# Two attention layers on one core: projections issued in halves over separate slots, the second transposes one slot after the norm, the router three slots earlier

## The reference, cut to what matters

```python
x = x + tanh(g_xattn[0]) * attention0(layernorm(x), ctx, mask)   # q from x, k and v from ctx
x = x + tanh(g_ffn[0])   * quantised_ffn(layernorm(x))           # fake-quantised, 768 wide
x = x + tanh(g_xattn[1]) * attention1(layernorm(x), ctx)
x = x + tanh(g_ffn[1])   * top1_moe(layernorm(x))                # 32 experts, 160 rows each
```

## Time and profile before

| | us |
|---|---|
| median of 3 executions | 1279.54 (1276.82 to 1281.15) |
| the profiled execution: its time | 1276.96 |
| its span, first to last instruction | 1275.7 |
| PE busy | 1202.8 (94% of the span) |
| DVE busy | 893.2 (70%) |
| ACT busy | 709.5 (56%) |
| POOL busy | 480.2 (38%) |

### The profile page before, as it was taken

The page is one execution under the profiler, slowest core; times in us unless marked ns, Lnnn a source line. Parts: engine busy times, 40 slices in busy tenths (PEclk is TensorE's granted clock), DMA queues, the critical chain, the costliest instruction groups (busy, mean ns, idle before and its releaser), DMA issues.

```text
span 1275.7 us, 25161 instructions
## 1 busy us (share of the span) xinstructions
PE 1202.8 (94%) x9252; PEld 861.7 (68%) x9252; DVE 893.2 (70%) x2680; ACT 709.5 (56%) x1197; POOL 480.2 (38%) x677
## 2 busy tenths in 40 slices
PE   7799999999999989999999998999999999989998
PEld 6567677767777664444448875777677677668987
DVE  4677777876787646589999955777877868652333
ACT  2355555555655538889984425666566666632221
POOL 5434434443443100057100434444544643323555
PEclk9899999999999989999999999999999999999999
DMA  7523334333432032000003654446456342148973
GB/s 187 136 61 111 96 93 117 89 101 99 125 92 68 11 108 76 1 1 2 1 1 116 173 149 121 128 114 183 126 163 150 106 132 83 52 147 253 306 193 36
DMA packets 121941, 137.22 MB, mean 108 GB/s; under 512 B 12881, under 2 KB 116427, under 8 KB 121797
## 3 DMA queue, kind: packets, MB, share of 16 engines
q1 hardware_dynamic: 111888, 125.98, 33.4%
q0 software_dynamic: 7296, 8.15, 3.5%
q10 hardware_dynamic: 2634, 1.49, 0.5%
HBM read 58.42 MB, written 27.36 MB: 67 GB/s over the span
## 4 chain that ended last, share of the span: by engine, by line
PE 56%; DVE 6%; issue 3%; ACT 2%; POOL 1%; DMA 1%; ACTq 0%; SPq 0%; POOLq 0%; DVEq 0%
PE PS L670 14%; PE PS L729 6%; PE PS L471 5%; PE PS L411 5%; PE PS L684 4%; PE PS L430 4%; PE PS L454 4%; PE PS L503 2%; PE PS L738 2%; PE PS L529 2%; PE PS L418 2%; DVE NM L1133 1%; PE PS L547 1%; ACT P L853 1%; PE PS L512 1%
## 5 line engine op out<-in xcount | busy, mean ns | idle before, releaser
L853 ACT ACTIVATE P<-PS 128x512 f32<-128x512 f32 x512 | 302.5, 602 | 162.5 <-PE PS L457 88.4
L1130 DVE CUSTOM_DVE_ANT_0 MX<-PS,NQ 128x256 bf16<-128x256 f32 x512 | 192.4, 418 | 72.1 <-PE PS L430 72.0
L454 PE MATMUL PS<-QS,KS 99*128 99x256 bf16 x1024 | 226.1, 274 | 8.1 <-ACT P L853 7.1
L1133 DVE TENSOR_REDUCE NM<-PS 128x2 f32<-128x512 f32 x256 | 173.6, 686 | 71.0 <-PE PS L430 69.4
L430 PE MATMUL PS<-KS,QS 96*128 96x256 bf16 x1024 | 196.4, 274 | 23.2 <-DVE NM L1130 14.7
L430 PEld LDWEIGHTS PS<-KS,QS 96*128 96x128 bf16 x1024 | 86.6, 97 | 89.0 <-DVE NM L1130 26.9
L471 PE MATMUL PS<-P,V 128*32 128x256 f32 x2048 | 138.4, 388 | 1.5 <-ACT P L853 1.5
L454 PEld LDWEIGHTS PS<-QS,KS 99*128 99x128 bf16 x1024 | 95.9, 99 | 50.7 <-ACT P L853 20.9
L457 PE MATMUL PS<-NK,identb 128*128 128x256 bf16 x512 | 128.0, 275 | 0.0
L670 PE MATMUL PS<-XNT,wup 128*128 128x512 f16 x576 | 124.9, 379 | 0.0
L670 PEld LDWEIGHTS PS<-XNT,wup 128*128 128x128 f16 x576 | 56.1, 98 | 67.4
(11 more groups left out here) (240 smaller groups left out, 2479.5 us busy)
## 6 DMA issues: line engine op xcount, KB each, us to landing
KS<-PP SPq DMA_DIRECT2D x192, 128.0 KB, 3.0
QS<-PP SPq DMA_DIRECT2D x192, 128.0 KB, 2.5
WH<-in_wex SPq DMA_DIRECT2D x16, 768.0 KB, 8.3
WG<-in_wex SPq DMA_DIRECT2D x10, 768.0 KB, 5.4
bufd<-bias_row SPq DMA_DIRECT2D x5, 1032.0 KB, 11.8
XB<-in_x SPq DMA_DIRECT2D x16, 256.0 KB, 3.1
CT<-in_ctxT SPq DMA_DIRECT2D x16, 256.0 KB, 3.1
x1d<-XB SPq DMA_DIRECT2D x16, 256.0 KB, 2.1
```

What stands on the lines that cost most here:

```text
L454: ins = tensor.matmul(o, t.KS[b % 3][0:99, h, 128 * kt:128 * kt + 128], t.QS[b % 3][0:99, h, :], start=True, stop=(L == 1))
L853: scalar.activation(t.P[h % 8][:, :, :], PS[:, h % 2, :].rearrange("p (k n) -> p k n", k=2), ACT.Exp).then_inc(s_ex, 1)
L1130: ins = vector.tensor_tensor_reduce(t.MX[:, 2 * (h % 2) + qt, :], PS[:, bk, 256 * qt:256 * qt + 256], t.NQ[b % 4][:, qt, :], -1.0, 1.0e30, ...
L1133: ins = vector.tensor_reduce(nm[:, :, h], PS[:, bk, :].rearrange("p (t n) -> p t n", t=2), X, ALU.max, negate=True)
```

## The change: what it does

For all sequences but the first two of a layer:

| job | slot before | slot after |
|---|---|---|
| keys | 0 | half in 0, half in 2 |
| rows | 1 | 3 |
| queries | 3 | half in 7, half in 8 |
| values | 13 | half in 12, half in 14 |
| DVE rounding of keys, queries | 2, 5 | 4, 10 |
| SP copies of the keys' parts | 2, 3 | 4, 5 |
| SP copies of the queries' parts | 4, 6 | 10, 11 |

For all sequences:

| job | slot before | slot after |
|---|---|---|
| out | 10 | half in 10, half in 11 |
| residual, statistics, moments | 10, 11, 12 | 11, 12, 13 |
| power on POOL | 12 | 13 |
| the two norm instructions | 13 and 14 | both in 14 |
| second transposes | 4 of the next but one `s` | 15 of the next `s` |
| router | 7 | 4 |
| heads | 5 and 6 | both in 6 (DVE: 6 and 7) |

Between its two halves a job keeps its bank, and the jobs between go to the other one. The preparation of the FFN's weights moves from slots 0, 3, 5 (of each 8) to 3, 4, 7. Before the experts, `pe_warm_mixed` becomes 30 of the plain unread matmuls. No arithmetic changes. The diff, cut to its core:

```diff
+def keys_at(b):
+    return (0, 0) if b < 2 else (0, 2)
+def rows_at(L, b):
+    return 3 if b >= 2 else 0 if rows_first(L, b) else 1
+def queries_at(b):
+    return (3, 3) if b < 2 else (7, 8)
+def values_at(b):
+    return (13, 13) if b < 2 else (12, 14)
+def mids_at(L, b):
+    return (4, 10) if b >= 2 else (2, 8 if (L, b) == (0, 1) else 5)
+def stacks_at(L, b):
+    return ((4, 5), (10, 11)) if b >= 2 else ((2, 3), (4, mids_at(L, b)[1] + 1))
...
-        def odd_bank(job, emptier, value):
+        def odd_bank(job, emptier, value, half=None):
+            if half == 1:
+                half_done.remove(home[job])
+                return home[job]
             turn[0] ^= 1
+            if 6 + turn[0] in half_done:
+                turn[0] ^= 1
             bk = 6 + turn[0]
+            if half == 0:
+                half_done.add(bk)
             if emptied[bk] is not None:
                 pe.wait_ge(*emptied[bk])
...
-                if k in (5, 6):
-                    pe_heads(L, s - 1, k - 5)
+                if k == 6:
+                    pe_heads(L, s - 1, 0)
+                    pe_heads(L, s - 1, 1)
...
-                    pe_out(L, s - 1)
+                    pe_out(L, s - 1, 0)
+                if k == 11:
+                    pe_out(L, s - 1, 1)
+                if k == 15:
+                    if s == NB:
+                        pe_warm(5, 14)
+                    pe_xm(L, s - 1)
             if 0 <= s - 2 < NB:
-                if k == 4:
-                    if s - 2 == NB - 1:
-                        pe_warm(5, 14)
-                    pe_xm(L, s - 2)
-                if L == 1 and k == 7:
+                if L == 1 and k == 4:
                     pe_router(s - 2)
...
-                if kk == 0:
+                if kk == keys_at(b)[1]:
                     act_split(L, b, 0)
+                if kk == rows_at(L, b) and not rows_first(L, b):
+                    act_xt(L, b)
...
-            if k == 13:
+            if k == 14:
                 dve.wait_ge(s_ers, n + 1)
...
                 dve_norm(x, out, st, 0)
-            if k == 14:
                 dve_norm(x, out, st, 1).then_inc(s_xm, 1)
...
-            if 0 <= s - 1 < NB and k == 12:
+            if 0 <= s - 1 < NB and k == 13:
                 pool_tail_rstd(L, s - 1)
...
-            pe_warm_mixed()
+            pe_warm(5, 30)
```

More of the change, by code:

```diff
@@ L7 @@
 F32 = mybir.dt.float32
-F32R = mybir.dt.float32r
 BF16 = mybir.dt.bfloat16
@@ L405, in col, with pe_project @@
             return sc[:, i:i + 1]
[L408 to L412, removed]
+        def pe_project(w, src, bk, mt):
+            for k in range(2):
+                ins = tensor.matmul(PS[:, bk, 256 * mt:256 * mt + 256], w[:, k, 128 * mt:128 * mt + 128], src[:, k, :],
+                                    start=(k == 0), stop=(k == 1))
             return ins
@@ L576, in pe_slot @@
                     continue
-                if kk == (0 if rows_first(L, b) else 1):
+                if kk == rows_at(L, b) and rows_first(L, b):
                     pe_xn(L, b)
-                if kk == 0:
[L580 to L586, removed]
+                for half in range(2):
+                    if kk == keys_at(b)[half]:
+                        pe_keys(L, b, half)
+                if kk == rows_at(L, b) and not rows_first(L, b):
+                    pe_xn(L, b)
+                for half in range(2):
+                    if kk == queries_at(b)[half]:
+                        pe_queries(L, b, half)
+                for half in range(2):
+                    if kk == values_at(b)[half]:
+                        if (L, b, half) == (0, 0, 0):
+                            pe_warm(5, 12)
+                        pe_values(L, b, half)
             if 0 <= s - 1 < NB:
@@ L617, in wq_step @@
         def wq_step(s, k):
[L619 removed]
+            return 3 * ((16 * s + k) // 8) + (3, 4, 7).index(k % 8) if s >= 0 and k % 8 in (3, 4, 7) else -1
         def wq_part(i, j):
@@ L693, in pe_warm @@
                 tensor.matmul(PS[:, bk, 0:128], ones[:, :], ident[:, :], start=True, stop=True)
[L695 to L706, removed]
         def pe_turn(e):
@@ L1712, in pool_slot @@
                     continue
-                if kk in (0, 3):
-                    pool_rest(L, b, int(kk == 3))
-                if kk in (2, mid_at(L, b)):
-                    pool_low(L, b, int(kk > 2))
+                for which, made in enumerate((keys_at(b)[1], queries_at(b)[1])):
+                    if kk == made:
+                        pool_rest(L, b, which)
+                    if kk == mids_at(L, b)[which]:
+                        pool_low(L, b, which)
             if 0 <= s + 3 < NB:
@@ L1890, in sp_slot @@
             for b, kk in heads_at(L, s, k):
-                for part in range(3):
-                    if kk == (2, 3, 3)[part]:
-                        sp_stack(L, b, 0, part)
-                    if kk == (4, mid_at(L, b) + 1, mid_at(L, b) + 1)[part]:
-                        sp_stack(L, b, 1, part)
+                for which in range(2):
+                    for part in range(3):
+                        if kk == stacks_at(L, b)[which][part > 0]:
+                            sp_stack(L, b, which, part)
             if 0 <= s - 1 < NB:
-                if L == 0 and k == 12:
+                if L == 0 and k == 13:
                     sp_x1(s - 1)
```

92 lines of the change are left out of this document (48 added, 44 removed).

## The result

The changed kernel takes 1335.97 us, the median of 4 runs (1334.16 to 1342.24), against 1279.16 for the kernel before on the same chip: a ratio of 1.045 [1.042, 1.049], 57 us slower. The forecast was 1315 and a range that ended at 1324. Both stalls that it named are there with the sizes it gave; the sum came out 20 us short.

A forecast was written before the change was run, and what follows sets the result against it. PE's own order was taken to bound the kernel. Layer 1 +25 us and 2 at its ends, layer 0 +9 and 2, together +38 on 1276.96, gave 1315 us; 8-in-10 range 1286 to 1324.

The forecast's parts named there:

- What bounds the kernel: Attention layers: PE's own order sets the pace, others matter where PE waits; an evener order wins at most some 33 us.
- First: rows wait for the bank of keys: Slot 3: rows wait for ACT's split of keys, 1.38 us in layer 1, 1.14 in layer 0; lower ends 0.9, 0.7.
- Second: second transposes wait for the norm: Slot 15: transposes wait for the chain from slot 13's scores to the norms, 1.2 us in layer 1, 0.8 in layer 0.
- Third: queries wait in slot 7: Slot 7: queries wait for DVE's scaling of heads, 0.2 us a sequence in layer 1, nothing in layer 0.
- What it removes: PE's long and empty slots: waits won back, 0.8 of 1.05 us a sequence in layer 1, 1.3 of 1.5 in layer 0.
- A lower clock: Unread matmuls before the experts: a lower clock for one stretch more could cost up to 1.7 us.
- at the ends: First and last sequences of each layer, slots shorter still in layer 1: another 2 us per layer.
- only one of the two binds: Rival: only the rows' or the second transposes' stall binds, 1279 to 1290, or both at lower ends, 1290 to 1302; chance 0.18.

The follow-up runs named there:

- e1_keys01: Changed kernel with the second half of keys in slot 1 instead of slot 2: 1303.2 us, ratio 1.020 to the kernel before.
- e10_third: Changed kernel with its two heads back in slots 5 and 6 on TensorE and VectorE: 1320.0 us, ratio 1.033 to the kernel before.
- e7_early_norm: Changed kernel with "out" whole in slot 10, the norm's chain a slot earlier, second transposes left in slot 15: 1310.1 us, ratio 1.028.
- e6_router7: e3_both with the router in slot 7 instead of slot 5: 1297.4 us, ratio 1.017 to the kernel before.
- e2_xm4: Changed kernel with second transposes back in slot 4 of the next but one sequence, router in slot 5, routing a slot later: 1305.2 us, ratio 1.021.
- e3_both: Changed kernel with the edits of both e1_keys01 and e2_xm4: 1283.5 us, ratio 1.005 to the kernel before.
- e5_heads56: e3_both with the two heads back in slots 5 and 6 instead of both in 6: 1258.75 us, ratio 0.988 to the kernel before.
- e4_warm30: Kernel before with only the unread matmuls before the experts changed, to 30 plain ones instead of the mixed stretch: 1282.1 us, ratio 1.002.
- e12_w136: e5_heads56 with mixed unread matmuls before the experts and layer 0's weights' jobs in slots 1, 3, 6 of eight: 1260.4 us, ratio 0.986.

## Why the prediction was right in sign and 20 us short

- **What bounds the kernel**: right. Everything found was a wait of PE in its own order, but for a few us of clock.
- **First: rows wait for the bank of keys**: right, 1.38 us in layer 1 as forecast and 1.2 in layer 0 (1.14), by the timeline; undoing it gave back 33 us (e1_keys01; 21.0 in the window of layer 1, some of it clock, and 12.8 in that of layer 0) where the term has 1.38 x 13 + 1.14 x 13 = 33. The Trainium skill (Perfetto Trace Analysis, Optimizing Tensor Performance) has independent matmul groups rotate through banks. This kernel rotates and stalls all the same, since a bank that is held between the two halves of a job leaves only one to rotate through. The 0.9 that the prediction set beside this rule as its lower end wasn't met.
- **Second: second transposes wait for the norm**: right, 1.27 for 1.2 in layer 1, about 1.0 for 0.8 in layer 0. With the transposes' place undone (31 us) it went, with the chain's (22 by the ratio) most of it. What the term missed: in one sequence of layer 0 it is 1.9, where DVE reduces a block of weights (114.57, 0.67 us) ahead of the maxima, and in two of layer 1 it is 2.2, as POOL issues DMAs ahead of the power:

```profile
954.58 0.97 POOL L1716 DMA_INDIRECT bufd<-XM,SLS  x1 [0.30 <-issue]
...
955.56 0.74 POOL L1691 TENSOR_TENSOR ST<-ST,mhalf 128x2 f32<-128x2 f32 x1
956.33 0.80 DVE L1199 TENSOR_SCALAR XM<-XNT,ST 128x256 f32<-128x256 f32 x2 [1.06 <-POOL ST L1691]
...
957.27 0.63 PE L452 MATMUL PS<-ident,XM 128*128 128x128 f32 x4 [2.00 <-DVE XM L1199]
```

- **Third: queries wait in slot 7**: this step failed by its size. Forecast 0.2 and 0, measured 0.5 and 0.25 in plain sequences (those without weights' jobs or the end of a router's group). There e10_third takes 24.44 us instead of 24.96 in layer 1, and 26.69 and 26.83 instead of 26.99 and 27.08 in layer 0. In sequences 4 and 10 of layer 0 the weights' jobs wait for the same heads (L689, 2.7 us in two) and "on" then for the queries' bank (2.4 us in two). Together 16 us (e10_third) where the term has 0.2 x 13 = 3. This is the largest error.
- **What it removes**: 0.8 in layer 1 was about right (0.9 is what is left when 24.96, the plain sequence after, is set against 22.67 before plus 1.4, 1.3 and 0.5); in layer 0 this step failed too. A plain sequence before shows just two waits there:

```profile
351.48 0.63 PE L418 MATMUL PS<-ident,ON 128*128 128x128 f32 x4 [0.33 <-DVE ON L1188]
...
354.60 0.39 PE L430 MATMUL PS<-KS,QS 96*128 96x256 bf16 x2 [0.28 <-DVE NM L1130]
```

With 0.17 more for each that is 0.95, and more than that could not go, where the term had 1.3. The sum then closes: 25.5 less 0.95, plus 1.2, 1.0 and 0.25 is 27.0, as measured. The mean of 1.5 us from the earlier trace rows included sequences with weights' jobs, and these did not win: 31.5 and 31.8 us after, 27.7 and 28.5 before. The missing 0.35 x 13 is 5 us.
- **A lower clock**: the forecast had at most 1.7 us before the experts, and no term for it elsewhere. In layer 1 the granted clock now falls to its lower level (1.2 of 2.4 GHz) for three short stretches, where the same stage has a mean of 1.00 before and 0.98 now. One inside such a stretch, then windows of one sequence each:

```profile
966.00:968.00 2.00, 2.00 (x18) 0.68 (x18) 0.02 (x1) 0.75 (x3) 1.16 (x1) 0.50 0.41 110
...
957.74:984.10 26.36, 23.96 (x195) 16.76 (x192) 17.23 (x41) 14.98 (x29) 9.44 (x15) 0.94 0.42 126
984.10:1009.06 24.96, 22.41 (x195) 16.28 (x193) 17.06 (x41) 14.96 (x29) 9.42 (x15) 1.00 0.44 129
...
1087.36:1114.03 26.67, 23.98 (x195) 16.75 (x193) 17.16 (x41) 15.08 (x29) 9.43 (x15) 0.94 0.31 90
```

The two with 0.94 are 1.4 and 1.7 longer than the one between, and a third, from 1009.06, 1.4 longer than its like at 905.73: 4.5 us. PE had stood for the 2.0 us shown at 957.27 before the first of them, but a stall of the same length at 1061.94 was followed by a window with 1.00. The same stage has two or three such stretches in the profiles of e10_third, e7_early_norm and e6_router7 too, and none in e1_keys01, e2_xm4, e3_both or e5_heads56. But e4_warm30, whose layer 1 is that of the kernel before, has two as well:

```profile
786.51:1089.61 303.10, 294.25 (x2511) 216.15 (x2512) 229.11 (x556) 191.88 (x379) 136.32 (x209) 0.99 0.46 128
```

That is 3.3 us more than in the earlier trace rows with no stall added. So a few us of what the experiments gave back may be clock, and that the stalls brought it down isn't shown.

The excess of 20 is thus about 13 from the third term, 5 from what is removed in layer 0, 4 from the clock, 5 from larger second stalls, less 2 at the ends. That makes 25, so they overlap by some 5 us, and the exact split stays open. No rival came true, "only one of the two binds" included.

That even slots win 10 to 15 us once the two stalls are gone, expected in e3_both, was false: the third loss and the router's wait were still in it, and small waits for ACT come back (5.7 us in 18). With these two undone as well (e5_heads56), 16 us are won. The fastest order, e5_heads56 (e12_w136 can't be told from it), is 1.2% faster than the kernel before, of which 9 us belong to the halves; the other 7 come with the other moves, and which of them wins them wasn't tried.

## What to carry to other kernels

Where jobs take turns in two buffers, list for each job which buffer it gets and who empties it; a job spread over several slots takes the turn away from all that stand between, and whoever comes next right behind it waits for its reader (e1, e6 and the earlier trace rows are the same stall at three places). Splitting long jobs wins 0.7% here, but what was moved along with them cost eight times that (5.8% between e5_heads56 and the changed kernel): re-derive each engine's queue order, the slow helper's (POOL) too, for every slot moved. Waits can't be added as terms of one sum once they share slack: removing two gave 52 of 64 us, and a third, priced at 5 to 8, gave 22.

## What was not expected of the hardware

A DMA issue on ACT's queue holds the ACT instructions behind it for 0.75 us (884.91 to 885.66, `ACTq` above). The changed kernel has 64 such issues of the maxima, 0.73 to 0.87 us each, and no ACT instruction starts during any of them.

One of DVE's norms takes 0.41 us. Beside a 128x512 instruction of POOL it takes longer. In the kernel before, with one norm:

```profile
120.76 1.05 POOL L1704 TENSOR_TENSOR w_nat<-w_nat,w_r 128x512 f32<-128x512 f32 x1 [0.90 <-DVE w_r L1304]
...
121.23 0.72 DVE L1163 TENSOR_SCALAR XM<-XB,ST 128x256 f32<-128x256 f32 x1
```

In e7_early_norm, with both norms in one row:

```profile
227.59 1.05 POOL L1737 TENSOR_TENSOR w_nat<-w_nat,w_r 128x512 f32<-128x512 f32 x1
...
227.75 1.35 DVE L1198 TENSOR_SCALAR XM<-XB,ST 128x256 f32<-128x256 f32 x2
```

In this row the first norm took 1.03 us and the second 0.40. The norm at 121.23 ends 0.14 us after POOL's instruction, and so do the first one of e7_early_norm and a third case in the kernel before (414.76, 0.54 us, beside POOL from 414.11 to 415.16). This made the second stall 1.0 us in one sequence of e7_early_norm where its neighbour had none. The Trainium skill (SBUF — State Buffer, SBUF: two separate sides) says that GpSimd shares a pair of ports with those DVE instructions that run in a two-port mode or have two SBUF inputs, as an exclusive lock, and that the loser waits for the whole instruction. The three cases agree: DVE, which started second each time, was done only when POOL's instruction had ended; whether it did part of its work beside it isn't shown.
